# Four normalizations of a decoder kernel: squares summed by fours instead of by pairs

## The reference, cut to what matters

```python
x = x + attn_ref(layernorm(x))          # mamba2, then gate/up/down
x = x + xattn_ref(layernorm(x), ctx)    # both operands quantized, then one product
x = x + ffn_ref(layernorm(x))           # weights w = base + coeff * sign(w - base)

def layernorm(x, axis=-1, eps=1e-05):
    m = mean(x); v = var(x)
    return (x - m) / sqrt(v + eps)

def fake_quant(x, scale, zp):
    return (clip(round(x / scale + zp), 0, 255) - zp) * scale
```

## Time and profile before

| | us |
|---|---|
| median of 3 runs | 2126.46 (2125.92 to 2126.57) |
| profiled execution | 2129.29 |
| its span in the trace | 2127.5 |
| TensorE busy | 2091.3 |
| VectorE busy | 1674.4 |
| ScalarE busy | 1060.2 |

### The profile page before, as it was taken

How to read it: one execution, slowest core, us unless ns; L and a number is a source line. 1 busy time by engine, 2 the same in 40 slices (tenths; PEclk the granted TensorE clock), 3 DMA queues, 4 the chain that set the end, 5 groups by cost and what they waited for, 6 DMA issues and landing times.

```text
span 2127.5 us, 26597 instructions
## 1 busy us (share of the span) xinstructions
PE 2091.3 (98%) x9254; PEld 1677.7 (79%) x9254; DVE 1674.4 (79%) x2516; ACT 1060.2 (50%) x1747; POOL 182.1 (9%) x296
## 2 busy tenths in 40 slices
PE   7998999999999999999999999999999999999999
PEld 4786778787888878888888854888888888888887
DVE  7877586797777888778979888987677776698885
ACT  5333244457777777774444366543333333444442
POOL 0001011101111211110000002000000000100000
PEclk9999999999999999999999999999999999999999
DMA  3151116639889999897340044554444443846101
GB/s 124 40 207 50 60 50 196 155 105 319 297 294 332 326 319 345 299 327 287 126 152 1 1 169 104 174 195 152 165 154 155 167 154 128 314 179 209 49 20 60
DMA packets 136433, 370.05 MB, mean 174 GB/s; under 512 B 16688, under 2 KB 27568, under 8 KB 132656
## 3 DMA queue, kind: packets, MB, share of 16 engines
q1 hardware_dynamic: 111216, 288.16, 39.3%
q0 software_dynamic: 25088, 80.23, 11.1%
HBM read 288.12 MB, written 84.41 MB: 175 GB/s over the span
## 4 chain that ended last, share of the span: by engine, by line
PE 85%; DVE 8%; ACT 3%; issue 2%; DMA 1%; SPq 0%; DVEq 0%; ACTq 0%
PE pair L1080 42%; PE pair L1105 25%; PE pair L852 7%; PE pair L1024 4%; DVE conv_out L2116 2%; PE pair L1138 1%; DVE pair L1933 1%; PE pair L962 1%; PE pair L983 1%; PE pair L876 1%; PE pair L1132 1%; DVE weights_lo L1699 1%; PE pair L845 1%; DMA ctx_in<-ctx 1%; PE pair L989 0%
## 5 line engine op out<-in xcount | busy, mean ns | idle before, releaser
L1080 PE MATMUL pair<-comb_hi,ring_hi 128*128 128x512 f32 x1456 | 567.6, 390 | 5.2 <-ACT gate_a L1413 5.2
L1080 PE MATMUL pair<-comb_hi,ring_lo 128*128 128x512 f32 x1456 | 567.1, 389 | 0.0
L1080 PE MATMUL pair<-comb_lo,ring_hi 128*128 128x512 f32 x1456 | 567.0, 389 | 0.0
L1105 PE MATMUL pair<-inner_ring_a,ring_hi 128*128 128x512 f32 x1120 | 344.9, 390 | 0.0
L1080 PEld LDWEIGHTS pair<-comb_hi,ring_hi 128*128 128x128 f32 x1456 | 273.5, 188 | 64.4 <-DVE ring_lo L1789 7.1
L1080 PEld LDWEIGHTS pair<-comb_hi,ring_lo 128*128 128x128 f32 x1456 | 273.5, 188 | 56.7
L1080 PEld LDWEIGHTS pair<-comb_lo,ring_hi 128*128 128x128 f32 x1456 | 273.5, 188 | 56.1
L1105 PEld LDWEIGHTS pair<-inner_ring_a,ring_hi 128*128 128x128 f32 x1120 | 210.3, 188 | 43.4
L1105 PE MATMUL pair<-inner_ring_a,ring_lo 128*128 128x512 f32 x560 | 218.1, 389 | 0.0
L1335 ACT ACTIVATE ring_hi<-ring_sum 128x512 fp32r<-128x512 f32 x160 | 101.1, 632 | 142.7 <-DVE ring_sum L1774 141.0
L1789 DVE TENSOR_TENSOR ring_lo<-raw_a,ring_hi 128x512 fp32r<-128x512 f32 x146 | 99.4, 685 | 52.1 <-ACT ring_hi L1335 52.1
(11 more groups left out here) (376 smaller groups left out, 3583.1 us busy)
## 6 DMA issues: line engine op xcount, KB each, us to landing
coeff_in<-f_gu SPq DMA_DIRECT2D x56, 512.0 KB, 5.1
coeff_in<-b_gu SPq DMA_DIRECT2D x56, 512.0 KB, 7.0
weights_raw<-w_mamba SPq DMA_DIRECT2D x44, 512.0 KB, 3.5
raw_a<-w_gu SPq DMA_DIRECT2D x28, 512.0 KB, 7.3
raw_a<-w_gu SPq DMA_DIRECT2D x56, 256.0 KB, 6.4
u_spill<-gate_a POOLq DMA_DIRECT2D x56, 256.0 KB, 5.8
coeff_in<-f_dn SPq DMA_DIRECT2D x28, 512.0 KB, 4.4
coeff_in<-b_dn SPq DMA_DIRECT2D x28, 512.0 KB, 6.3
```

The costliest lines, as they stand in the source:

```text
L1080: ins = pe.matmul(out, wt[:, slot, col], a, start=t in (0, 1, 3) and kk == 0 and n == 0, stop=kk == KH - 1 and n == 2, skip_group_check=True)
L1105: ins = pe.matmul(out, wt[:, slot, col], a, start=t in (0, 1, 3) and k == 0 and n == 0, stop=k == SC_PAIRS - 1 and n == 2, skip_group_chec ...
```

## The change

For e = 2, 3 and 4, VectorE adds the pair sums 0 and 1, and 2 and 3, once more, so that TensorE multiplies two tiles instead of four. The adds of pairs there are followed by `own.then`, as the third add reads what they wrote; the third releases `s_hpair`. The four variances' counts (`VAR_DONE`) follow. ScalarE's squares of e = 4, which overwrite the tiles of e = 3, wait for the product of their group of four. For e = 5 the same three pairs and two single squares stay.

```diff
-    VAR_DONE = {1: KT, 2: KT + KH, 3: KT + 2 * KH, 4: KT + 3 * KH, 5: KT + 3 * KH + 5}
+    VAR_DONE = {1: KT, 2: KT + 2, 3: KT + 4, 4: KT + 6, 5: KT + 11}
...
-        def ctx_var(out, square, pairs, pair_count, alone, square_count):
-
-            for n, j in enumerate(pairs):
-                pe.wait_ge(s_hpair, pair_count + n + 1)
-                pe.matmul(out, ones_mean[:, :], square(2 * j), start=n == 0, stop=not alone and n == len(pairs) - 1).then_inc(s_hvar, 1)
+        def ctx_var(out, square, firsts, sum_count, alone, square_count):
+
+            for n, k in enumerate(firsts):
+                pe.wait_ge(s_hpair, sum_count + n + 1)
+                pe.matmul(out, ones_mean[:, :], square(k), start=n == 0, stop=not alone and n == len(firsts) - 1).then_inc(s_hvar, 1)
...
-        ctx_var(bank(1), x_square_a, range(KH), 2 * KT, (), 0)
+        ctx_var(bank(1), x_square_a, (0, 4), 2 * KT, (), 0)
...
-        ctx_var(bank(7), x_square, range(KH), 2 * KT + KH, (), 0)
+        ctx_var(bank(7), x_square, (0, 4), 2 * KT + 2, (), 0)
...
-        ctx_var(bank(7), x_square, range(KH), 2 * KT + 2 * KH, (), 0)
+        ctx_var(bank(7), x_square, (0, 4), 2 * KT + 4, (), 0)
...
-        ctx_var(bank(7), x_square, range(3), 2 * KT + 3 * KH, (6, 7), 5 * KT)
+        ctx_var(bank(7), x_square, (0, 2, 4), 2 * KT + 6, (6, 7), 5 * KT)
...
-                act.wait_ge(s_hvar, VAR_DONE[2 + b] + k // 2 + 1)
+                act.wait_ge(s_hvar, VAR_DONE[2 + b] + k // 4 + 1)
...
-        def square_pairs(e, square, pairs):
-            for j in pairs:
-                dve.wait_ge(s_hsq, e * KT + 2 * j + 2)
-                TT(square(2 * j), square(2 * j), square(2 * j + 1), ALU.add).then_inc(s_hpair, 1)
+        def square_pair(e, square, k):
+            dve.wait_ge(s_hsq, e * KT + k + 2)
+            return TT(square(k), square(k), square(k + 1), ALU.add)
+
+        def square_sums(e, square, firsts):
+            for k in firsts:
+                own.then(square_pair(e, square, k))
+                own.then(square_pair(e, square, k + 2))
+                TT(square(k), square(k), square(k + 2), ALU.add).then_inc(s_hpair, 1)
...
-        square_pairs(2, x_square_a, range(KH))
+        square_sums(2, x_square_a, (0, 4))
...
-        square_pairs(3, x_square, range(KH))
+        square_sums(3, x_square, (0, 4))
...
-        square_pairs(4, x_square, range(KH))
+        square_sums(4, x_square, (0, 4))
...
-        square_pairs(5, x_square, range(3))
+        for k in (0, 2, 4):
+            square_pair(5, x_square, k).then_inc(s_hpair, 1)
```

## The result

| | before | changed |
|---|---|---|
| median of 13 runs, us | 2127.13 | 2131.99 |
| profiled span, us | 2127.5 | 2130.4 |

The ratio of the two is 1.0019, interval 1.0011 to 1.0027: 4.0 us slower (2.3 to 5.7), inside the 0.2% named in the prediction. The forecast was +3.9 and 2130.4, its range 2126.6 to 2132.3; 2131.99 lies in it, near its upper end, as these 13 runs of before have a median 0.7 us above the 2126.46 that the forecast started from.

The account below looks back on a forecast made before the run. Between the feed-forwards TensorE, though 98% busy, was taken to wait for VectorE and ScalarE at the changed places. Queues +2.45 us and a clock fall +1.5 gave 3.95, say 3.9, on 2126.46: 2130.4 us, range 2126.6 to 2132.3.

Parts of the forecast that it names:

- Sums of queues, up to e = 2: At e = 2 VectorE's longer set delays everything up to L1182 by 1.67 us; TensorE waits 1.2 and 1.1.
- The wait's price: On VectorE, an add that the next one waits for takes 0.72 us instead of 0.60: 0.12 us per wait.
- Rival 2: On VectorE waits cost nothing, a set grows by 1.2 us; 2.65 us slower in all, 2129.1; chance 0.08.
- e = 3: Idle time absorbs most of this set's growth: column terms 2.60 us later, Ln of the root 1.85 later.
- Rival 3: At all three sets idle time absorbs nothing: 5.0 us plus 1.5 for the clock, 6.5 slower, 2132.9; chance 0.12.
- e = 4: VectorE's row work comes late, so TensorE idles 2.4 us before L1143, which starts 2.45 us later than before.
- The sum of the queues: Delay of TensorE accumulated over the three sets, e = 2 to 4, through waits on other engines: +2.45 us.
- The clock's 1.5 us: Behind the new 2.4 us gap before L1143 TensorE's clock falls to 1.2 GHz, adding 1.5 us.
- Rival 1: Same queues, but no clock fall behind the gap before L1143, or an old fall goes: +2.45 us, 2128.9; chance 0.25.
- Rivals 4 and 5: At the sets: removed products make up VectorE's lateness, 2126.5, chance 0.06; or TensorE is the bound, 2121.1, chance 0.04.

Follow-up runs that it names:

- spread: The whole change, but VectorE does a set's four pair adds first, then the two adds of sums; one run, 2132.21 us against 2127.95 before.
- before_rows_first: The kernel before, pairs everywhere, with the mean rows at e = 4 computed ahead of the weights; ratio to before 0.9997.
- e4_only: The kernel before with only e = 4 summed by fours, e = 2 and 3 keeping pairs; one run, 2132.62 us against 2127.95 before.
- after_filled: The whole change plus two fp32 products that nobody reads, ahead of `ctx_var` e = 5 on TensorE; ratio to before 1.0016.

## Why the prediction was right

- Sums of queues, up to e = 2: right. A set grows by 1.70 (forecast 1.67), L1182 moves by 1.70, TensorE waits 1.07 and 0.93 for the sums (1.2 and 1.1).
- The wait's price: 0.12 us in the row, 0.12 on the chip. Rival 2 falls: `spread` saves 0.49 where it would save nothing. But the prediction went too far where it held the row to contradict the Trainium skill, "VectorE: DVE Perf Modes", section "The DRAIN you can't avoid". The Trainium skill reports there that a semaphore after each operation costs nothing; it does not say that the next operation waited for it. Raising one is free here too: the pair adds of before each raise `s_hpair` and stand 0.60 us apart. The 0.12 is what it costs to wait at once.
- e = 3: right against the profile that I had, column terms +2.65 (2.60), Ln +1.89 (1.85), and wrong as a statement of the kernel. The step that failed is the slack that I let the set's growth fall into: VectorE's 0.67 us before L2335 and ScalarE's 0.66 before the Ln, both ended by TensorE. TensorE was late there for the slow clock at L1185, which the six other profiles with pairs at e = 2 do not have. In `before_rows_first` both waits are gone, and the third, VectorE's 1.47 before the rsqrt, which the prediction counted too, is 0.68. So the set of e = 3 comes through whole, 1.70 instead of the 0.18 that the sum gave it. Rival 3 had this: "It decides wherever a wait that I took as slack has two releasers." For e = 4 and for its total of 6.5 it was wrong.
- e = 4: right. L2345 is the releaser of L1143, the gap is 2.27 (2.4), the cost alone 0.64 (0.60 in the sum); taking L2345 forward removes it.
- The sum of the queues was thus 3.9 and not 2.45: 1.70 + 1.70 + 0.64 less a tenth. That alone would be the measured 4.0, if the clock cost both kernels the same.
- The clock's 1.5 us: wrong as a term, as what it named did not happen in the profile. It is not excluded as such: behind a gap of 2.3 to 2.5 us before L1143 the clock stayed up in two profiles (the changed kernel, `e4_only`) and fell in two (`after_filled`, `spread`). In the first profile it stayed up behind the new gap and was low for 6.8 instead of 3.4 us at e = 5, which made e = 5 to `second_mean` 7.48 instead of 6.16; the old fall behind L1161 went, but the 1.6 us that TensorE gained on the profile of before in the first 25 records were lost again by about 1363 us, as its weight loads now waited for VectorE, 1.3 us for `comb_lo` and 0.9 for `ring_lo`. So a fall right at the start of the second feed-forward costs nothing here. In other executions the falls lie elsewhere: in the changed kernel itself, and in variants of before that are the same code up to there. What the clock adds on average is open: the changed kernel's mean granted clock is lower by 0.002, while the queues alone come within 0.1 us of the ratio's 4.0, whose interval is 1.7 us either way.
- So the total agreed with the forecast by luck: a set that I had sized 1.5 us too small and a clock term of 1.5 that did not come made up for each other. The mechanism, VectorE's longer sets reaching TensorE through three handovers, was right.
- Rival 1, the same queues without a fall behind the gap, had the clock of the first profile right and shares the e = 3 that was sized too small.
- Rivals 4 and 5 fall: at e = 2 and 3 the removed products gave nothing back. At e = 4 TensorE was the bound before, but the longer set handed the bound to VectorE's L2345, so there they gave 1.71 us back only once the mean rows came first.

## What to carry to other kernels

An engine that is busy 98% can still be late for others' sake in the stretch that a change touches: read who releases it there before you count its saved instructions. A slack found in one profile is to be asked who made it; here a slow clock in one execution had made 1.5 us of it, and none of six further profiles with the same order up to there had it. A second profile of the kernel before would most likely have shown that. And a sum that comes out right does not vouch for its terms. Look first for work that stands ahead of the awaited instruction without need: with it moved, a third of the same edit, at e = 4, was part of a kernel that beat before.

## What the runs showed of the hardware

An add that waits for a semaphore which the add right before it raises started 0.72 us after that one; with another add between the two, every add started 0.60 us after its neighbour (128x512 fp32; the changed kernel and `spread`). Waits of 0.77 and 0.93 us behind 64 one-column products were followed by 13.7 us at 1.2 GHz in one execution of the changed kernel. Gaps ahead of L1143 were followed by none where they took 2.27 us (changed) and 2.28 (`e4_only`), by 3.4 us where 2.28 (`after_filled`), and by 10.2 where 2.52 (`spread`). So in these profiles the length of a gap did not tell whether the clock fell behind it.
